# TensorE's loop over groups begins at the third step's output products in place of the first transposes

## What is computed

```python
x = x + attn(cond(x, itok_B_0_7, weights, fside))      # x: 64 x 64 x 512
x = x + ffn(cond2(x, W, A, Bm, scalings, itok_B_0_6))

# attn, latent size L = 128, 16 heads, per batch row of 64 tokens
h = x @ WA + bA;  kv_lat, q_lat = split(h)
kRt, qRt = rope(h @ WB + bB), rope(h @ WC + bC)
scores = ([q, qRt] . [k, kRt]) * dk ** -0.5            # q = q_lat @ WUQ, k = kv_lat @ WUK
attn = softmax(where(causal, scores, -inf))
out = (attn @ v) @ WZ + bZ                             # v = kv_lat @ WUV
# ffn: four experts, the best two per token, gelu between W1 and W2
```

## Time and profile before

| | |
|---|---|
| median of 3 runs | 1929.16 us (1926.45 to 1935.68) |
| the profiled execution | 1927.72 us |
| its span, first to last instruction | 1925.6 us |
| TensorE busy | 1825.1 us, 95% |
| VectorE, ScalarE, GpSimd busy | 48%, 33%, 37% |
| mean granted TensorE clock | 0.985 of full speed |

### The profile page before, as it was taken

One profiled execution on the slowest core, in us unless ns is written; L12 is line 12 of the kernel. 1 busy time (PEld: TensorE's weight loads), 2 busy tenths in 40 slices (PEclk: granted clock), 3 DMA queues, 4 the chain that ended last, 5 costly groups with the idle time before them and its releaser, 6 DMA issues. The chain is left out here.

```text
span 1925.6 us, 29419 instructions
## 1 busy us (share of the span) xinstructions
PE 1825.1 (95%) x10664; PEld 1418.1 (74%) x10664; DVE 922.9 (48%) x1581; ACT 627.2 (33%) x1088; POOL 705.7 (37%) x525
## 2 busy tenths in 40 slices
PE   6899999999999999999999997999999999999996
PEld 4577676777767677677777776888888888888884
DVE  4565656556565665656433683242424232333321
ACT  4333333333333333333223112333333333333331
POOL 1232223223221222322100033565757575757563
PEclk9999999999999999999999998999999999999998
DMA  7000101010010100102033115033304230422011
GB/s 259 23 1 17 51 6 62 1 42 26 17 51 6 62 1 29 39 17 61 17 120 110 50 66 191 22 71 106 85 0 109 87 65 0 131 87 44 6 16 22
DMA packets 68588, 104.81 MB, mean 54 GB/s; under 512 B 12304, under 2 KB 29456, under 8 KB 68496
## 3 DMA queue, kind: packets, MB, share of 16 engines
q1 hardware_dynamic: 53568, 76.92, 12.2%
q0 software_dynamic: 7200, 16.78, 4.9%
q10 hardware_dynamic: 7728, 9.71, 1.4%
HBM read 78.23 MB, written 25.17 MB: 54 GB/s over the span
## 5 line engine op out<-in xcount | busy, mean ns | idle before, releaser
L1861 DVE CAST hh<-hid 128x512 fp32r<-128x512 f32 x128 | 92.6, 723 | 453.3 <-ACT hid L1806 453.3
L1731 POOL TENSOR_TENSOR w1l<-w_raw,w1h 128x512 fp32r<-128x512 f32 x112 | 185.3, 1654 | 153.4 <-ACT w1h L1798 153.3
L441 POOL TENSOR_TENSOR prob<-prob,rinv 128x512 f32<-128x512 f32 x64 | 66.7, 1043 | 460.1 <-DVE rinv L700 460.1
L95 PE MATMUL bank_o<-Mh,mix_h 128*128 128x512 f32 x512 | 211.6, 413 | 2.3 <-DVE mix_l L671 1.4
L95 PE MATMUL e_h<-xh,w1h 128*128 (+1 forms) x512 | 203.5, 397 | 5.6 <-POOL w1l L1731 5.6
L97 PE MATMUL e_h<-xh,w1l 128*128 (+1 forms) x512 | 202.7, 396 | 0.0
L96 PE MATMUL e_h<-xl,w1h 128*128 (+1 forms) x512 | 202.7, 396 | 0.0
L97 PE MATMUL bank_o<-Mh,mix_l 128*128 128x512 f32 x512 | 202.6, 396 | 0.0
L96 PE MATMUL bank_o<-Ml,mix_h 128*128 128x512 f32 x512 | 202.2, 395 | 0.0
L95 PE MATMUL e_y<-w2h,hh 128*128 128x512 f32 x512 | 201.2, 393 | 0.0
L96 PE MATMUL e_y<-w2l,hh 128*128 128x512 f32 x512 | 200.6, 392 | 0.0
(11 more groups left out here) (303 smaller groups left out, 3486.3 us busy)
## 6 DMA issues: line engine op xcount, KB each, us to landing
w_raw<-in_W_dram SPq DMA_DIRECT2D x56, 512.0 KB, 4.2
stage<-in_x_dram SPq DMA_DIRECT2D x8, 1024.0 KB, 6.3
x_res<-in_x_dram SPq DMA_DIRECT2D x32, 256.0 KB, 3.2
out_dram<-x_res SPq DMA_DIRECT2D x32, 256.0 KB, 2.0
flat_dram<-flat_sb ACTq DMA_DIRECT2D x32, 256.0 KB, 2.0
rows<-out_dram SPq DMA_DIRECT2D x4, 1024.0 KB, 5.4
stage<-in_W_dram SPq DMA_DIRECT2D x8, 512.0 KB, 5.6
x_res<-out_dram SPq DMA_DIRECT2D x3, 1024.0 KB, 5.2
```

The source lines that it names most:

```text
L95: nc.tensor.matmul(out, ah, bh, start=start and n == 0, stop=False)
L441: nc.gpsimd.tensor_tensor(prob[:, i % 2, :, :], prob[:, i % 2, :, :], rinv[:, :].unsqueeze(2).to_broadcast([P, HB, C]), ALU.mult).then_inc ...
L1731: nc.gpsimd.tensor_tensor(w1l[:, k, :, :], w1_at(pair, chunk), w1h[:, k, :, :].bitcast(F32), ALU.subtract).then_inc(S["w1_lo"], 1)
L1861: nc.vector.tensor_copy(hh[:, k, :], hid[:, k, :]).then_inc(S["h_hi"], 1)
```

## The change

The part of TensorE's body from prob_transpose(g, 0) to prob_transpose(g, 3) becomes a function of its own, front. It is called for group 0 ahead of the loop, and for group g + 1 at the end of the body of group g; the last body, written out, has no front. TensorE thus does the same work in the same order; the loop's top and the jump back lie between prob_transpose(g, 3) and the output product of step 2. The other engines' loops stay where they were.

```diff
                 scores(0, 0, first=True)
                 scores(0, 1)
                 kv_tokens(0)
-
-            def body(g, more):
+                front(0)
+
+            def front(g):
                 prob_transpose(g, 0)
                 scores(g, 2)
                 mix(g, 0)
...
                 scores(g, 4)
 
                 prob_transpose(g, 3)
+
+            def body(g, more):
+
                 wz(g, 2, range(HB))
                 mix(g, 3)
                 scores(g, 5)
...
                     scores(g + 1, 1)
                     kv_tokens(g + 1)
                     wz(g, 7, range(HB))
+                    front(g + 1)
                 else:
                     wz(g, 4, range(HB))
                     prob_transpose(g, 6)
```

## The result

The changed kernel takes 1966.6 us (median of 6 runs, 1963.0 to 1967.9) against 1929.87 us for the kernel before, run beside it: ratio 1.0185, 95% interval 1.0171 to 1.0199, 36.7 us slower. The profiled execution has a span of 1965.8 us, 40.2 more than before.

What follows compares the result with a forecast made beforehand. TensorE, busy 95% of the span, was taken to bound the kernel; -8.8 (old gap) + 33.6 (new jump) + 7 (clock) = +31.8 us on the profiled 1927.72, so 1961 us for the timed median, range 1940 to 1968.

Steps and rivals of the forecast that it cites:

- The edge and the two gaps: At the new jump: instruction-piece edge 10 instructions behind the loop's top, two fetches, 5.6 us lost a jump, 33.6 for six.
- The target's packet: Fetch of the instruction piece the jump aims at: put 0.7 us after the moment the first product now starts.
- The second gap: After four products behind the jump, TensorE waits about 2.5 us for the next instruction piece.
- the first gap: Behind the jump, ahead of the first bank_o product: about 3.1 us (0.7 + 2.4) for the target piece.
- The removed gap: Instruction wait in the bank_s scores (line 887) behind the old jump back: goes, -8.8 us in six.
- The clock: TensorE's granted clock falls behind the new jump at four of six jumps: 7 us, bounds 0 and 10.3.
- The sum: Whole kernel: -8.8 + 33.6 + 7 = +31.8 us on the profiled 1927.72; 1961 us for the timed median.
- B: Rival: one fetch instead of two at the new jump, only 3.1 us x 6 stays; +13, 1942 us; chance 13%.
- A: Rival: the fetch at the new jump is hidden by long products, the 8.8 us go; 1920.4 us; chance 7%.
- C: Rival: time unchanged, another gap of about 1.5 us replaces the old one at the jump; 1929 us; chance 7%.

Runs made afterwards that it cites:

- the fill: Seven unread 128x512 matmuls in the rotation's wait: 1916.02 us with step 2's products ahead of the loop, 1915.58 in the kernel before plus 30 wait instructions, 1962.4 in the changed kernel.
- 202 pads: Kernel before with 202 instructions that only wait for a semaphore long reached, at the start of TensorE's program: 1937.52 us, ratio 1.0046.
- 191 pads: Changed kernel with 191 instructions that only wait for a semaphore long reached, at the start of TensorE's program: 1955.41 us, ratio 1.0121.
- 20 pads: Changed kernel with 20 instructions that only wait for a semaphore long reached, ahead of the loop: 1925.48 us, ratio 0.9977.

## Why the prediction was right, and where it was off

**The edge and the two gaps: right.** An edge 10 instructions behind the top meant four products between two gaps, and all six jumps show four. The target's packet starts a mean 0.55 us behind the moment at which the first product would have started, 0.41 us behind the transposes (predicted 0.7); the products start 2.7 us later (2.4), and the fifth stands a mean 6.23 us behind that moment (6.6) in place of 1.0. Lost: 5.2 us a jump, 31.4 for six; predicted 33.6. The second gap is 1.03 us, not 2.5, and little of that is a gain: the fifth product starts 2.7 to 3.2 us behind the first (3.5 by the forecast), and at five of the six jumps the clock had already fallen in the first gap, so that the four products fill more of this time (they start 0.43 us apart, not 0.23). The second piece comes 3.1 to 3.5 us after the target's; at the old place it was 3.0 to 3.6 over the six jumps, and not 3.6 each time, as I wrote.

**The removed gap: right.** bank_s with "issue" is gone. The rotation's wait is 1.0 us longer over all groups (24.2 against 23.2), and no other wait of TensorE in the groups grew by more than 0.3 us.

**The clock: the term that was mis-sized.** I put 7 us, four falls of 1.71, with 10.3 as the upper bound. A group with the loop kept and no fall takes 111.1 us. Before, a group takes 113.35: 1.47 are the gap, the other 0.8 I put down to the clock, though the trace shows only two falls of 1.7 in these six groups, which is 0.6. After, it takes 119.6, 8.5 more than 111.1: 5.2 are the late fifth product, 1.3 the falls behind the rotation's wait (five of six groups by 1.57), which leaves 2.0 for half clock behind the jump. Clock after less clock before is 1.3 + 2.0 - 0.8 = 2.5 us a group, 15 us in all, above my upper bound too. Two things failed: I counted one fall of 1.71 for a jump, and the trace shows 3.4 of granted clock missing at five jumps and 5.1 at one, part of it inside the gap; and I took the falls behind the rotation's wait as given, though they came in four more groups. Why the clock falls there in nearly every group after, and in few before, is not settled; the fill shows only that this wait is where it starts. The wait alone doesn't decide it: in the kernel before with 202 pads, seven waits of 1.9 to 2.0 us were followed by a single fall. One of the others there:

```profile
237.63 0.50 PE L95 MATMUL bank_p<-lat_h,Ah 128*128 128x512 f32 x1 [1.96 <-ACT rope_raw L519]
...
237.00:247.00 10.00, 9.37 (x43) 7.22 (x44) 6.88 (x16) 5.70 (x11) 2.80 (x2) 1.00 0.01 2
```

**The sum.** -8.8 + 31.4 + 15 = 37.6 us against 36.7 by the medians; I had +31.8. The gaps were 2 us too dear and the clock 8 us too cheap. The term for the clock is what the other terms leave of a group's growth (six times 119.61 - 113.35 is 37.6), so the sum is no check of it. The spans differ by 40.2; the other 2.6 us lie ahead of the first group, whose token transposes begin at 89.07 in place of 86.44 us, in code that the change leaves as it was.

**The rivals.** B (only the first gap stays) didn't come, as the count of the edge was right. Where an edge far behind the top was made, its picture came in part: with 191 pads only the first gap stands, at the three jumps that fetch; with 20 pads both vanish, since the loop is kept. A's time, 1920, was within reach, but by a way that I didn't name: the loop is not fetched at all, and the wait for the rotation is filled. C has nothing for it. What the prediction lacked is the question in front of all three: do the loop's pieces fit at once? The count that answers it was in the earlier trace rows: TensorE's program of before is 25.5 pieces long, and 79 packets are 54 more than one pass through it needs.

## What to carry to other kernels

If a loop's engine shows idle time by "issue" behind its jump back, count the instruction packets first: if they grow with the rounds, the loop isn't kept, and what helped here is fewer pieces, by where its top lies (shorter code should do the same, which no run here tests). Where a loop has to be fetched, an edge far behind its top and a queue of products ahead of its jump nearly hid the fetch. A move that changes no work still moves addresses; here 20 do-nothing instructions were worth some 40 us. Idle time of TensorE costs twice where the clock falls behind it, and a wait that can't be shortened can be filled with matmuls that nobody reads.

## What was not expected of the hardware

- A loop of 1625 instructions is kept when it touches seven pieces of 256 and fetched whole in every round when it touches eight: 25 packets against 79. With eight pieces of which the last holds 14 instructions, both happened in one execution (53 packets), and every round was fetched where products were queued ahead of the jump (80 packets).
- Seven products of 128x512 in a wait of 1.96 us keep the granted clock at full speed behind it, where it otherwise read half for 3.4 us (1.7 us lost). In the kept loop that is worth 10 us by the medians, from 1926 to 1916 (7 to 9 by the ratios to the kernel before, as these runs were not made side by side), and gives the fastest versions here: 1915.58 and 1916.02 us, ratios 0.9943 and 0.9932.
